# Later stages' loads, masks and first norms moved ahead of them, one barrier at each boundary, first loads on two queues

## The reference, cut

```python
xn = layernorm(x); x = x + L0_attn(xn) + L0_ffn(xn)   # 16 causal heads of 8; fp8 GEMM
xn = layernorm(x); x = x + L1_attn(xn) + L1_ffn(xn)   # chunked linear attention; low-rank gelu
xn = layernorm(x); x = x + L2_attn(xn) + L2_ffn(xn)   # 8 heads summed; tree of 256 leaves
xn = layernorm(x); x = x + L3_attn(xn) + L3_ffn(xn)   # Mamba block; 6 layers of local attention + GLU
```

## Time and the profile before

| | |
|---|---|
| Median of 3 runs | 4949.91 us (4947.79 to 4951.49) |
| The profiled execution, its own time | 4954.48 us |
| Its span, first to last instruction | 4953.2 us |
| Mean granted clock of TensorE | 0.977 |
| Stages in the trace, PE's first row to the last residual's end | L0 33.05 to 495.39, L1 517.79 to 695.59, L2 709.67 to 1132.10, L3a 1151.78 to 1641.39, L3f from 1648.70 |

### The profile page before, as it was taken

One profiled execution on the slowest core, in us unless ns is written; L12 is line 12 of the kernel. 1 busy time (PEld: TensorE's weight loads), 2 busy tenths in 40 slices (PEclk: granted clock), 3 DMA queues, 4 the chain that ended last, 5 costly groups with the idle time before them and its releaser, 6 DMA issues.

```text
span 4953.2 us, 115870 instructions
## 1 busy us (share of the span) xinstructions
PE 4669.7 (94%) x45088; PEld 3168.2 (64%) x45088; DVE 3438.3 (69%) x4939; ACT 3509.7 (71%) x6742; POOL 3707.7 (75%) x2336
## 2 busy tenths in 40 slices
PE   6999789996888699999999999999999999999997
PEld 4665558884444366666666666666666666666665
DVE  4553446665999677777777777777777777777774
ACT  2443655554777478778888888888877888887885
POOL 1111224445999789999999999999999999999993
PEclk9999889997999899999999999999999999999999
DMA  0000000002343222232222222232223222222222
GB/s 23 2 1 1 7 14 1 1 1 112 139 170 137 58 62 53 65 78 61 63 65 67 69 65 62 54 82 66 54 65 78 61 64 65 67 69 65 61 54 50
DMA packets 163477, 288.98 MB, mean 58 GB/s; under 512 B 44143, under 2 KB 60278, under 8 KB 158838
## 3 DMA queue, kind: packets, MB, share of 16 engines
q1 hardware_dynamic: 161926, 281.18, 21.6%
q10 hardware_dynamic: 1008, 0.39, 0.0%
HBM read 90.09 MB, written 2.62 MB: 19 GB/s over the span
## 4 chain that ended last, share of the span: by engine, by line
PE 64%; ACT 1%; POOL 1%; issue 1%; DVE 1%; DMA 0%; ACTq 0%; DVEq 0%
PE ps L2461 21%; PE ps L2519 8%; PE ps L2493 8%; PE ps L2474 7%; PE ps L2532 7%; PE ps L2506 4%; PE ps L2558 3%; PE ps L2574 3%; PE ps L2565 2%; PE ps L2488 2%; PE ps L2545 1%; PE ps L2539 1%; POOL L3f_t L3049 0%; POOL L3f_raw L3066 0%; DMA L3f_qks<-in_L_ffn_k_scale 0%
## 5 line engine op out<-in xcount | busy, mean ns | idle before, releaser
L3049 POOL TENSOR_TENSOR L3f_t<-L3f_raw,L3f_rot 128x512 f32<-128x512 f32 x768 | 1100.7, 1456 | 291.3 <-DVE L3f_raw L2876 288.8
L2461 PE MATMUL ps<-L3f_wqkv,all_z 128*128 128x512 f32 x2304 | 1171.9, 608 | 31.1 <-DVE L3f_raw L2876 22.4
L3066 POOL TENSOR_TENSOR L3f_raw<-L3f_raw,L3f_t 128x1024 f32<-128x1024 f32 x384 | 954.8, 2487 | 3.8
L3058 POOL TENSOR_TENSOR L3f_raw<-L3f_raw,L3f_rot 128x1024 f32<-128x1024 f32 x384 | 910.1, 2370 | 3.8
L2876 DVE TENSOR_TENSOR L3f_raw<-ps,L3f_ri 128x512 f32<-128x512 f32 x768 | 507.2, 682 | 273.6 <-ACT L3f_ri L2683 250.2
L2859 DVE TENSOR_REDUCE L3f_ss<-L3f_sqr 128x8 f32<-128x512 f32 x768 | 510.3, 679 | 218.3 <-ACT L3f_sqr L2673 217.1
L2704 ACT ACTIVATE L3f_qz<-ps 64x512 f32<-64x512 f32 x768 | 450.8, 587 | 179.0 <-PE ps L2474 174.4
L2474 PEld LDWEIGHTS ps<-all_ident,L3f_raw 128*128 128x128 f32 x3072 | 371.1, 141 | 293.7 <-issue 263.8
L2461 PEld LDWEIGHTS ps<-L3f_wqkv,all_z 128*128 128x128 f32 x2304 | 386.7, 191 | 263.4 <-issue 165.2
L2673 ACT ACTIVATE L3f_sqr<-ps 128x512 f32<-128x512 f32 x768 | 452.5, 596 | 67.7 <-PE ps L2461 61.3
L2725 ACT ACTIVATE L3f_pT<-ps 64x512 f32<-64x512 f32 x768 | 454.0, 591 | 55.4 <-PE ps L2506 46.4
(11 more groups left out here) (342 smaller groups left out, 8564.9 us busy)
## 6 DMA issues: line engine op xcount, KB each, us to landing
L3f_vw<-L3f_v SPq DMA_DIRECT2D x1344, 128.0 KB, 2.4
L3a_Bs<-L3a_rows SPq DMA_DIRECT2D x16, 2048.0 KB, 7.1
L3a_Cs<-L3a_rows SPq DMA_DIRECT2D x16, 2048.0 KB, 11.6
L3f_vw<-L3f_v SPq DMA_DIRECT2D x192, 64.0 KB, 2.1
L3f_wqkv<-in_L_ffn_Wqkv SPq DMA_DIRECT2D x24, 256.0 KB, 2.8
L3f_wqkv<-in_L_ffn_Wqkv SPq DMA_DIRECT2D x6, 512.0 KB, 3.6
L3f_wo<-in_L_ffn_Wo SPq DMA_DIRECT2D x48, 64.0 KB, 2.3
out<-all_x SPq DMA_DIRECT2D x8, 256.0 KB, 3.1
```

The lines of the kernel that those rows point to most:

```text
L2461: p.matmul(PS[:, j % 3, :], Z[:, u % NSEQ, t * P:t * P + P], w, start=True, stop=True).then_inc(proj.sem)
L3049: op = g.tensor_tensor(t[:, :, to], r[:, :, fr], w[:, 1, to].unsqueeze(1).broadcast_to((P, H, WIN)), ALU.mult)
L3058: g.tensor_tensor(r, r, w[:, 0, :].unsqueeze(1).broadcast_to((P, H, HD)), ALU.mult).then_inc(cosined.sem)
L3066: g.tensor_tensor(r, r, t, ALU.add).then_inc(rotated.sem)
```

## The change

Each stage becomes a generator with several `yield`s, held in a `Part`; `go_on(n)` writes the next piece of stage `n`. Pieces of later stages are written into the loop of earlier ones by `between`. At `k == -2` of L0 all later stages issue their first DMAs, some 80 on SP (and L3a's seven small memsets on POOL). At `k == 6` of L0 POOL sets `Z` to zero and does L1's memsets, ACT L3a's exponential, and DVE L1's masks, L3a's twelve preparations and L3f's centring matrix, rotation table and mask. At `k == NSEQ - 1` of each stage, one or two steps before its loop ends, the first norms of the next stage are written. At a boundary only one barrier is left, and SP clears behind it while the others go on. The table loads of L1's, L2's, L3a's and L3f's heads are gone.

At the start X comes as two DMAs, 4 sequences first and the rest behind L0's weights; ident and eight small loads are issued on the ACT queue; `Wp` comes padded from the host in one DMA instead of 16; L0's first three steps of ACT, DVE and POOL are written ahead of `prepare` (the DVE preparations). Only the quantised GEMM waits for `kq`.

```diff
+    def between(self, n, k):
+        if n == 0 and k == -2:
+            for later in range(1, len(self.parts)):
+                self.go_on(later)
+        if n == 0 and k == 6:
+            self.nc.gpsimd.memset(self.Z[:, :, :], 0.0)
+            for later in range(1, len(self.parts)):
+                self.go_on(later)
+        if k == NSEQ - 1:
+            self.go_on(n + 1)
+
+    def leave(self, n):
+        nc, part = self.nc, self.parts[n]
         nc.all_engine_barrier()
-        for s in self.raised:
+        for s in part.raised:
             nc.sync.sem_clear(s.sem)
-        self.raised = []
-        nc.all_engine_barrier()
+        part.buffers.close()
+        if n:
+            self.parts[n - 1].sems.close()
...
-            nc.sync.dma_start(self.X[:, :, :], d["L0_attn_x"].rearrange("b (t p) d -> p (b t) d", p=P)).then_inc(got_x.sem, 16)
-            nc.sync.dma_start(self.ident[:, :], d["c_ident"]).then_inc(got_ident.sem, 16)
...
-            nc.gpsimd.memset(self.Z[:, :, :], 0.0)
...
-            nc.sync.wait_ge(got_x.sem, 16)
-            nc.all_engine_barrier()
...
+        nc.sync.dma_start(self.X[:, 0:FIRST * TILES, :], x[:, 0:FIRST * TILES, :]).then_inc(self.got_x.sem, 16)
+        nc.scalar.dma_start(self.ident[:, :], d["c_ident"]).then_inc(self.got_ident.sem, 16)
+        nc.gpsimd.memset(self.eps[:, :], EPS).then_inc(self.got_eps.sem)
+        for n in reversed(range(len(self.parts))):
+            self.go_on(n)
+        nc.sync.dma_start(self.X[:, FIRST * TILES:, :], x[:, FIRST * TILES:, :]).then_inc(self.got_rest.sem, 16)
+        for n, part in enumerate(self.parts):
+            self.part = part
+            for _ in part.steps:
+                pass
+            if n + 1 < len(self.parts):
+                self.leave(n)
...
     def L0(self):
...
+            v.wait_ge(*self.got_ident.at(0, 15))
+            v.wait_ge(got_w.sem, NW * 16)
...
-        load()
-        nc.all_engine_barrier()
...
+        nc.vector.wait_ge(*self.got_x.at(0, 15))
+        nc.gpsimd.wait_ge(*self.got_x.at(0, 15))
+        nc.scalar.wait_ge(*self.got_eps.at(0))
+        for k in range(-5, -2):
+            act(k)
+            dve(k)
+            pool(k)
+        prepare()
+        nc.vector.wait_ge(*self.got_rest.at(0, 15))
+        nc.gpsimd.wait_ge(*self.got_rest.at(0, 15))
+        for engine in (nc.tensor, nc.scalar, nc.gpsimd):
+            engine.wait_ge(*w_ready.all(0))
+        for k in range(-2, NSEQ + 2):
             pe(k)
             act(k)
             dve(k)
             pool(k)
-        self.settle()
+            self.between(0, k)
...
     def L1(self):
...
-        nc.sync.wait_ge(got_w.sem, NW * 16)
-        nc.all_engine_barrier()
...
+        before = self.parts[0].x_done
+        nc.vector.wait_ge(*before.at(2))
+        nc.gpsimd.wait_ge(*before.at(2))
+        for k in range(-5, -2):
+            act(k)
+            dve(k)
+            pool(k)
+        yield
```

More of the change, by code:

```diff
@@ L38, in row, with __init__ @@
     return ap.rearrange("(a n) -> a n", a=1).broadcast_to((P, n))
+class Part:
+    def __init__(self, tag, steps):
+        self.tag, self.steps = tag, steps
+        self.buffers, self.sems, self.raised = ExitStack(), ExitStack(), []
 class Kernel:
     def __init__(self, nc, d, out, stages):
-        self.nc, self.d, self.out, self.stages = nc, d, out, stages
+        self.nc, self.d, self.out = nc, d, out
+        programs = {"L0": self.L0, "L1": self.L1, "L2": self.L2, "L3a": self.L3a, "L3f": self.L3f}
+        self.parts = [Part(tag, programs[tag]()) for tag in stages]
     def sb(self, name, shape, dt=F32):
-        return self.ctx.enter_context(self.nc.sbuf_tensor(f"{self.tag}_{name}", shape, dt))
+        return self.part.buffers.enter_context(self.nc.sbuf_tensor(f"{self.part.tag}_{name}", shape, dt))
     def signals(self, *names):
@@ new lines, in L0 @@
+        for to, fr in ((fbias[:, :], row(d["L0_ffn_bias"], P)), (lsel[:, :], d["c_lsel"]), (wp[:, :, :], d["L0_attn_Wp_T"])):
+            nc.sync.dma_start(to, fr).then_inc(got_w.sem, 16)
+            NW += 1
+        nc.scalar.preload_act_table_set(EXP_LN)
+        nc.gpsimd.memset(vz[:, :, :, :, :], 0.0).then_inc(zeroed.sem)
+        nc.gpsimd.memset(mxe[:, :, :], 0.0).then_inc(zeroed.sem)
+        nc.gpsimd.wait_ge(*zeroed.at(0, 0))
+        for b in range(2):
+            for t in range(TILES):
+                for u in range(2):
+                    op = nc.gpsimd.memset(vz[:, b, t, :, 48 * u + HD:48 * u + HD + 1], 1.0)
@@ L1623, in pool @@
             left(k + 1)
-        nc.scalar.preload_act_table_set(EXP_LN)
-        for k in range(-3, NSEQ + 1):
-            pe(k)
+        before = self.parts[1].x_done
+        nc.vector.wait_ge(*before.at(2))
+        nc.gpsimd.wait_ge(*before.at(2))
+        for k in range(-3, -1):
             act(k)
@@ L2234, in pool @@
             xm_(k + 3, 0)
+        before = self.parts[2].x_done
+        nc.vector.wait_ge(*before.at(2))
+        nc.gpsimd.wait_ge(*before.at(2))
+        for k in range(-4, -2):
+            act(k)
+            dve(k)
+            pool(k)
+        yield
+        xg = self.sb("xg", [P, CH * SEQ])
+        zg = self.sb("zg", [P, CH * SEQ])
+        de = self.sb("de", [P, CH * SEQ])
+        xc = self.sb("xc", [P, 2, CH, SEQ])
+        zs = self.sb("zs", [P, 2, CH * SEQ])
+        dt = self.sb("dt", [P, 2, CH, SEQ])
+        dx = self.sb("dx", [P, 2, CH, SEQ])
+        Bs = self.sb("Bs", [P, 2, NS, SEQ])
+        Cs = self.sb("Cs", [P, 2, NS, SEQ])
+        db_x = self.sb("db_x", [P, NX, G, SEQ])
+        hs = self.sb("hs", [P, G, SEQ])
+        hc = self.sb("hc", [P, 2, CH, G, SEQ])
+        yT = self.sb("yT", [P, CH, SEQ])
+        nc.tensor.wait_ge(*made.all(0))
+        nc.scalar.wait_ge(*made.all(0))
         for k in range(-4, NSEQ + 1):
@@ new lines, in L3f @@
+        nc.sync.dma_start(lmask, d["c_local"]).then_inc(got_m.sem, 16)
+        load_small(0)
+        load_wo(0)
+        load_w1(0)
+        load_w2(0)
+        yield
+        nc.gpsimd.memset(mean[:, :], 1.0 / P).then_inc(made.sem)
+        nc.vector.memset(floor, 1e-24).then_inc(made.sem)
+        nc.vector.wait_ge(*self.got_ident.at(0, 15))
+        nc.vector.tensor_scalar(cmat[:, :], ident[:, :], -1.0 / P, None, ALU.add).then_inc(made.sem)
+        nc.vector.wait_ge(*got_c.at(0, 15))
+        rotation(0)
```

408 lines of the change are left out of this document (198 added, 210 removed).

## The result

The changed kernel took 4899.59 us (median of 4 runs, 4893.87 to 4901.63), beside 4950.7 for the kernel before (4 runs): a ratio of 0.9888, interval 0.9863 to 0.9912. It is faster by 51 us; 79 were forecast, and the time lies outside the stated range. In the profiled executions the spans differ by 55.6 us (4953.2 and 4897.6).

What follows compares the result with a forecast made beforehand. PE, busy 94% of the span, was taken as the bound, with time to win only where it stands still. Terms -22.0, -20.7, -13.8, -16.8, -11.5 and +5.5 sum to -79.3: 4871 us, range 4857 to 4887.

Steps and rivals of the forecast that it cites:

- what is put in at `k = 6`: L0: added DVE rows and POOL memsets delay `lower` beyond its 2.2 us slack, stopping PE; +5.5 us, bounds 0 and 9.
- Rival 2: More gained than summed: clock not halved after short gaps (4.5 us), `k = 6` block perhaps only 1; 4861, chance 0.12.
- rival 4: Whole kernel slower than before through a lower mean granted clock; at 0.955 it would be 4975; chance 0.03.
- the signs of being wrong: Clears delaying a barrier, work inside a stage taking another time, or PE's mean clock differing by more than 0.002.
- The memset's hold on DVE: L0, `k = 6`: POOL's 3.5 us Z memset may block DVE's row at 271.28; PE +5.6 with it, +4.5 without.
- The start: Before L0: smaller first X load and earlier norm let PE start near 11.0 instead of 33.05; -22.0 us.
- the second queue: Start: eight loads issued on the ACT queue save only issue time, 8 of half a microsecond, 4 us.
- Boundary 0 to 1: L0 to L1: PE starts at 497.1 instead of 517.79, including +1.4 from the norm ahead of a product; -20.7 us.
- 1 to 2: Boundary L1 to L2: next stage starts at 695.9 instead of 709.67; -13.8 us.
- 2 to 3a: Boundary L2 to L3a: gap shrinks by 19.4, less 2.6 for a delayed copy of probabilities; -16.8 us.
- 3a to 3f: Boundary L3a to L3f: first product at 1647.4 instead of 1658.89; -11.5 us.
- the rivals: Five other outcomes: start yields half, more gained, new waits, slower, change ineffective; chances 0.16, 0.12, 0.06, 0.03, 0.03.

Runs made afterwards that it cites:

- three kernels with the norm behind: Changed kernel with L1's and L3a's first norms behind their boundaries, 4896.91 us; that plus work in pieces, late X wait and later kq, 4871.07 and 4871.02 us.
- the two kernels with doses: Kernel before plus four DVE memsets of a spare tile in L0, of 3600 to 7200 columns, then of 3900 to 4800: 5023.61 us and 5023.78 us.
- the kernel with two barriers: Changed kernel with the second barrier behind SP's semaphore clears put back at each boundary: 4907.44 us.

## Why the prediction was wrong

**The step that failed** is the cost of what is put in at `k = 6`: "I take **+5.5** ... bounds 0 and 9". It was 23.4: 3.0 in the period before (29.09) and 20.4 in the next (46.56). The stop was of the forecast size. DVE's block took 5.7 us, 5.9 were forecast, and PE stood still for 1.8 us and 4.1, 5.9 in all. What I put at nothing is what comes behind the stop: PE runs on at half its clock, and that cost some 17 us. Shown: the same work without the stop gave 23 us back, and stops without the work, seven of them from 1.59 us up, cost 16 to 17 each besides themselves.

Some of this was to be seen in the rows: the earlier trace rows have the clock at 0.50 or 0.87 at the two boundaries that they show. I read it as a thing of the boundaries. Rival 2 used it as a gain and rival 4 as a loss over the whole kernel, and neither priced what one stop brings; the kernel's own fall of the clock at 464, behind stops of 1.00 and 1.22 us, stands nowhere in the working. Of the signs of being wrong "the work inside a stage takes another time" came true, while PE's mean clock hardly differed (0.977 and 0.976 in the two profiled executions): the mean over the span didn't show it.

**The memset's hold on DVE** was the right mechanism with too small a size. The row held up (L190, the one ahead of the row that was forecast) took 4.99 us, not 3.5, since POOL's next memset followed without a gap; with Z's memset alone it took 4.11. The page "SBUF — State Buffer" of the Trainium skill says in "Who interferes with whom" that DVE and GpSimd share a pair of ports, that whoever issues first has it for the whole instruction, and that the other is blocked until then. This trace agrees as to the blocking: the row ended 0.15 us behind a memset in both kernels. It doesn't agree as to the order, as the DVE row's start is shown 0.44 us ahead of the memset's, and the row was held through two memsets. No run here took the lock away by itself. The hold cost 3.0 us in its period; moved to `k = 9`, without L1's memsets, it cost 2.1, of which the next period gave back 1.0.

**The start:** forecast -22.0, found -20.7 at the first residual. The transposes were right to 0.1 us. I covered the wait for the rest of X with PE's work alone and missed that ACT's first copy is queued behind it. That delayed the first projection by 3.6 us, and PE's earlier return to the full rate gave 2.3 of it back. (Without the wait `kq` is next in line, and only 1.6 of the 3.6 are to be had.) By the rule of the page "DMA: Bandwidth & Descriptors" of the Trainium skill, "Issuing engines are not separate DMA queues", the prediction had 4 us for the second queue; the trace has 3.8.

**Boundary 0 to 1:** forecast -20.7, found -18.7. The gap was right (0.48). The end of L0 grew by 3.2 and not 1.4: 2.3 as the norm stands ahead of the product (7.84 instead of 5.55), and 0.9 in the last step, all of which PE ran at half clock, in the kernel before only from 491.5 on. The first part was gone in all three kernels with the norm behind; the last step took 5.55, 7.15 and 6.47 in them (6.46 in the kernel before), so the second part isn't the norm's.

**The other boundaries** were right within 0.6 us: 1 to 2, -13.5 (-13.8); 2 to 3a, -16.2 with the copy delayed (-16.8); 3a to 3f, -10.9 (-11.5). For 2 to 3a that close a match is in part luck, as L2's length scatters by 5 us from trace to trace. L1 and L3f took 0.9 and 0.8 us longer, which no term had.

With 23.4 for 5.5 the forecast sum would have been -61.4, and with the 1.3 of the start, the 1.8 of L0's end and the 1.7 of L1 and L3f -56.6, against the -55.6 of the traces. None of the rivals was this, and the range ended at 4887, since I had bounded this term at 9.

## What to carry to other kernels

Where PE runs without a break, look up how much slack it has behind the engine you add work to, and keep every piece of added work under it. Here seven stops of 1.6 to 5 us at one place cost 16 to 17 us each besides themselves, whatever their length, and one of 1.3 cost only itself. Which stops do this has to be looked up for each kernel, in the granted clock behind the stops that its trace already has.

Cut work hoisted ahead of a boundary into pieces and lay them into several steps. That goes for memsets too, as a long one on POOL held up DVE's tensor_scalar for as long as it ran.

The four gaps shrank by 65.5 us in all. Clearing semaphores behind one barrier was 10.6 of them. The loads, masks, memsets and table loads were never taken apart, so how the rest divides among them isn't shown. Hoisting the first norms of L1 and L3a into tails whose engines wait in a chain gave nothing that these runs show.

## What of the hardware was not expected

- After a stop of PE of 1.28 us the granted clock stayed at 1.00. After stops of 1.59 us and more at the same place, seven of them in the two kernels with doses, it went to 0.50 and stayed there for 34 to 38 us, though PE was busy all the time from its restart on. The stops of 2.5 to 4.1 us at `k = 6` of the changed kernel and its variants did the same, but for the kernel with two barriers, where it was 24 us.
- The length of the stop alone doesn't decide: one of 1.77 us ahead of L419 left the clock at 1.00, and stops of 1.00 and 1.22 us, 1.4 us of work apart, were followed by 17 us at 0.50 at the end of L0 in the kernel before.
- Where the low clock lasted 34 to 38 us it came back at the same place of L0's step, in or just behind the products with the probabilities (L406, rows of 128x256; about 275 us in the changed kernel). Why there, and why elsewhere and sooner in the kernel with two barriers, stays open.
- A DVE tensor_scalar that took 0.64 us in other periods took 4.99 beside a row of POOL memsets, 4.11 beside the one of 3.52, 1.87 beside shorter ones (1.77 us in all) and 1.10 beside one of 0.52.
